# A transformer block on one core: feed-forward groups interleaved on VectorE, rounding constants made by ScalarE, the last group rounded in halves

## What is computed

```
x = x + attention(layernorm(x) * gamma + beta)     # x: 4 x 1024 x 128, 16 heads of 64
y = layernorm(x)
gate, up = q(y) @ q(w_gate).T, q(y) @ q(w_up).T    # 128 -> 352, twice
h = silu(gate) * up
x = x + q(h) @ q(w_down).T                         # 352 -> 128
```

## Time and profile before

| what | us |
| --- | --- |
| median of 3 runs (1539.41 to 1540.51) | 1540.29 |
| profiled execution, its own time | 1539.5 |
| its span, first to last instruction | 1537.7 |
| PE busy | 1458.0 (95%) |
| DVE busy | 1159.8 (75%) |
| ACT busy | 896.4 (58%) |
| POOL busy | 1346.2 (88%) |
| mean granted PE clock (1 is 2.4 GHz) | 0.983 |

### The profile page before, as it was taken

How to read it: one execution, slowest core, us unless ns; L and a number is a source line. 1 busy time by engine, 2 the same in 40 slices (tenths; PEclk the granted TensorE clock), 3 DMA queues, 4 the chain that set the end, 5 groups by cost and what they waited for, 6 DMA issues and landing times.

```text
span 1537.7 us, 28203 instructions
## 1 busy us (share of the span) xinstructions
PE 1458.0 (95%) x10537; PEld 771.2 (50%) x10537; DVE 1159.8 (75%) x1566; ACT 896.4 (58%) x1384; POOL 1346.2 (88%) x789
## 2 busy tenths in 40 slices
PE   4799999999999999999999999999999999997677
PEld 2345555555555455555555455555555455553455
DVE  7887777777777777777778777777777778754786
ACT  1366666666666666766566666666666656663222
POOL 3599999889889899999889899999889899975774
PEclk9899999999999999999999999999999999999898
DMA  5211121112111121111211111122112111100001
GB/s 142 48 37 49 36 50 50 41 50 49 49 45 33 45 50 35 50 41 49 49 49 45 36 43 49 36 50 48 42 50 50 45 45 33 31 25 16 7 14 35
DMA packets 69207, 67.26 MB, mean 44 GB/s; under 512 B 26512, under 2 KB 52432, under 8 KB 69072
## 3 DMA queue, kind: packets, MB, share of 16 engines
q1 hardware_dynamic: 69072, 65.46, 17.0%
HBM read 29.25 MB, written 2.62 MB: 21 GB/s over the span
## 4 chain that ended last, share of the span: by engine, by line
PE 87%; DVE 8%; issue 2%; ACT 2%; POOL 1%; DMA 0%; SPq 0%; ACTq 0%; DVEq 0%; POOLq 0%
PE po L1169 28%; PE st L1156 24%; PE mx L1217 11%; PE ms L1197 8%; PE ms L1234 4%; PE ms L1182 4%; PE ms L1245 4%; PE ms L1225 1%; PE mx L1304 1%; PE st L1304 1%; DVE probs L848 1%; DVE negmax L893 1%; DVE st L842 1%; POOL psum_keys L398 1%; DVE probs L1061 1%
## 5 line engine op out<-in xcount | busy, mean ns | idle before, releaser
L398 POOL TENSOR_TENSOR psum_keys<-psum_keys,probs 128x1024 f32<-128x1024 f32 x256 | 610.0, 2383 | 72.8 <-ACT probs L659 50.6
L659 ACT ACTIVATE probs<-st 128x1024 f32<-128x1024 f32 x512 | 497.5, 1028 | 122.3 <-PE st L1156 117.9
L893 DVE TENSOR_REDUCE negmax<-mx 128x2 f32<-128x1024 f32 x322 | 393.4, 1222 | 121.3 <-PE mx L1217 121.0
L1169 PE MATMUL po<-probs,v 128*64 128x512 f32 x2048 | 483.5, 593 | 0.0
L895 DVE TENSOR_REDUCE negmax<-mx 128x1 f32<-128x512 f32 x186 | 128.6, 692 | 183.4 <-PE mx L1217 183.4
L1169 PEld LDWEIGHTS po<-probs,v 128*64 128x64 f32 x2048 | 141.7, 137 | 218.9 <-issue 164.3
L1217 PE MATMUL mx<-keys_hi,queries_hi 64*128 64x512 f32 x1016 | 231.6, 452 | 13.8 <-DVE negmax L893 6.9
L1156 PE MATMUL st<-queries_lo,keys_hi 64*128 64x512 f32 x1024 | 201.9, 391 | 0.0
L1156 PE MATMUL st<-queries_hi,keys_hi 64*128 64x512 f32 x1024 | 201.7, 390 | 0.0
L1156 PE MATMUL st<-queries_hi,keys_lo 64*128 64x512 f32 x1024 | 201.7, 391 | 0.0
L1217 PEld LDWEIGHTS mx<-keys_hi,queries_hi 64*128 64x128 f32 x1016 | 95.8, 185 | 167.1 <-issue 124.8
(11 more groups left out here) (173 smaller groups left out, 1770.2 us busy)
## 6 DMA issues: line engine op xcount, KB each, us to landing
kq<-sin_part SPq DMA_DIRECT2D x256, 128.0 KB, 2.4
rsum<-recips SPq DMA_DIRECT2D x128, 128.0 KB, 2.9
wqkv<-in_L_attn_w_qkv_dram SPq DMA_DIRECT2D x32, 192.0 KB, 2.8
resid<-in_L_attn_x_dram SPq DMA_DIRECT2D x4, 512.0 KB, 8.1
wout<-in_L_attn_w_out_dram SPq DMA_DIRECT2D x32, 64.0 KB, 2.6
out_dram<-resid SPq DMA_DIRECT2D x8, 256.0 KB, 2.3
sums<-sums_kept SPq DMA_DIRECT2D x64, 4.0 KB
spread<-sums SPq DMA_DIRECT2D x64, 4.0 KB, 1.5
```

The lines of the kernel that those rows point to most:

```text
L398: nc.gpsimd.tensor_tensor(psum_keys[:, c], first, probs[:, (STEPS * P + i) % RING], ALU.add)\
L659: nc.scalar.activation(probs[:, step_n % RING], st[step_n % 2][:, :], ACT.Exp, scale=SCALE)\
L893: nc.vector.tensor_reduce(out, banks[:, :], AX.X, ALU.max, negate=True).then_inc(mx_free, 1)
L1169: last = mm(po[HD * a:HD * a + HD, :], v[:, P % 2, KEY_ORDER[jt], HD * a:HD * a + HD], probs[:, step_n % RING, a], start=(jt == 0), stop=( ...
```

## The change

- VectorE: the tiles of group g + 1 are put between the steps of group g: two tiles, the scales of g, two tiles, the values and exponents of g. The residual of group g - 3 is added before the scales.
- The exponents of h are a `tensor_tensor` with a mask column in PSUM (`h_mask`), broadcast over the columns, in place of a `tensor_scalar` with an immediate.
- The rounding constants of h are made by ScalarE with two instructions, `Relu(e - 1)` and `ROUND_C * that + ROUND_C`, whose biases are columns in SBUF (`rounding`). ScalarE signals `h_val_done`. In its queue they are the last thing of the next group.
- There are two tanh tiles in place of four, and four h buffers in place of three. `down` runs three groups behind in place of two, in halves of two tiles with `gate_and_up` of the next group between them; three groups of it are left at the end in place of two.
- `last_y` and `y_evac` of groups 6 and 7 move to between the halves of `down` in groups 5 and 6. `normalise_y` moves from ACT's group 2 to group 3, `maxima_y` and `reciprocals_y` behind the values of groups 2 and 3, and `last_exponents(7)` behind those of group 4.
- Group 7 is rounded by VectorE in two halves of 704 columns, and PE's last `down` starts after the first.
- The second reciprocal of pair 31 is taken before tiles 2 and 3 of group 0.

```diff
-    tanh_all = probs_flat[:, 0:GT * FFN]
-    h_all = [probs_flat[:, (1 + r) * GT * FFN:(2 + r) * GT * FFN] for r in range(3)]
+    tanh_tiles = [probs_flat[:, i * FFN:(i + 1) * FFN] for i in range(2)]
+    h_all = [probs_flat[:, 2 * FFN + r * GT * FFN:2 * FFN + (r + 1) * GT * FFN] for r in range(4)]
...
+    last_exp = st[1][:, :].rearrange("p c n -> p (c n)")[:, 0:2 * FFN]
+    h_mask, h_round = (halves[0][:, 2 * PART + i:2 * PART + i + 1] for i in range(2))
...
+        def constants_h(g, q):
+            if g == 0:
+                act.wait_ge(rounding_done, 1)
+            act.wait_ge(h_exp_done, g + 1)
+            nc.scalar.activation(h_exp[q], h_exp[q], ACT.Relu, bias=rounding[:, 0:1]).then_inc(h_two_done, 1)
+            act.wait_ge(h_two_done, g + 1)
+            nc.scalar.activation(h_exp[q], h_exp[q], ACT.Identity, bias=rounding[:, 1:2], scale=ROUND_C)\
+              .then_inc(h_val_done, 1)
+
         def group(g, q):
             gate_tanh(g, (2, 3))
-            if g == 2:
+            if g > 2:
+                copy_hT(g - 3, (0, 1))
+            if g in (GROUPS - 3, GROUPS - 2):
+                y_evac(g + 1)
+            if g == 3:
                 normalise_y(GROUPS - 2)
                 normalise_y(GROUPS - 1)
             if g < GROUPS - 1:
                 gate_tanh(g + 1, (0, 1))
-            if g > 1:
-                copy_hT(g - 2)
+            if g > 2:
+                copy_hT(g - 3, (2, 3))
+            if g > 0:
+                constants_h(g - 1, 1 - q)
...
+        def values(g, q):
+            link(scaled(h_all[g % 4], h_all[g % 4], GT * FFN // BLOCK, h_recip))
+            wide = [PART, GT * FFN]
+            nc.vector.tensor_tensor(h_exp[q].bitcast(I32), h_all[g % 4].bitcast(I32),
+                                    h_mask.bitcast(I32).broadcast_to(wide), ALU.bitwise_and).then_inc(h_exp_done, 1)
+
+        def own_rounding(g, q):
+            n = 2 * FFN
+            dve.wait_ge(h_exp_done, GROUPS)
+            link(nc.vector.tensor_scalar(h_amax, h_scale[:, q], 1.0, None, ALU.mult))
+            for half in range(2):
+                cols, blocks = slice(half * n, half * n + n), slice(half * n // BLOCK, (half + 1) * n // BLOCK)
+                link(nc.vector.scalar_tensor_tensor(last_exp, h_exp[q][:, cols], 1.0, h_round.broadcast_to([PART, n]),
+                                                    ALU.max, ALU.mult))
+                round_and_scale(h_all[g % 4][:, cols], last_exp, h_amax[:, blocks], n // BLOCK).then_inc(h_own_done, 1)
...
+        def group(g, q):
             if g < GROUPS - 1:
-                rounding_constants(h_exp[q]).then_inc(h_val_done, 1)
-            else:
-                link(rounding_constants(h_exp[q]))
+                gated(g + 1, (0, 1))
+            if g == 1:
+                output_half(1)
+            if g > 2:
+                add_residual(g - 3)
+            scales(g, q)
+            if g < GROUPS - 1:
+                gated(g + 1, (2, 3))
+            if g == 0:
+                filled(dve, ("S", PAIRS - 1, 1))
+            values(g, q)
+            if g == GROUPS - 1:
+                own_rounding(g, q)
                 add_residual(g - 2)
-                round_and_scale(h_all[g % 3], h_exp[q], h_scale[:, q], GT * FFN // BLOCK).then_inc(h_own_done, 1)
             if g == 1:
                 seed_shift(ln_rstd, batch_rows(BATCH - 1), BATCH + 2)
                 seed(ln_rstd, batch_rows(BATCH - 1))
+            if g == 2:
+                maxima_y(GROUPS - 2)
+                maxima_y(GROUPS - 1)
+            if g == 3:
+                reciprocals_y(GROUPS - 2)
+                reciprocals_y(GROUPS - 1)
             if g == 3:
                 last_exponents(GROUPS - 2)
+            if g == 4:
+                last_exponents(GROUPS - 1)
...
-        over_groups(gated)
+        gated(0, (0, 1))
+        nc.vector.memset(h_mask.bitcast(I32), EXPONENT)
+        nc.vector.memset(h_round, ROUND_C)
+        link(nc.vector.memset(rounding[:, 0:1], -1.0))
+        nc.vector.memset(rounding[:, 1:2], ROUND_C).then_inc(rounding_done, 1)
+        reciprocals(PAIRS - 1, 1)
+        gated(0, (2, 3))
+        output_half(0)
+        over_groups(group)
...
         def group(g, q):
             gate_and_up(g, (2, 3))
...
+            if g == 0:
+                output_projection(PAIRS - 1, 0)
+            if g > 2:
+                down(g - 3, (0, 1))
+            if g in (GROUPS - 3, GROUPS - 2):
+                last_y(g + 1)
             if g < GROUPS - 1:
                 gate_and_up(g + 1, (0, 1))
-            if g > 1:
-                down(g - 2)
+            if g == 1:
+                output_projection(PAIRS - 1, 1)
+                read_out(pe, ("O", PAIRS - 1, 1))
+            if g > 2:
+                down(g - 3, (2, 3))
...
-        down(GROUPS - 2)
-        down(GROUPS - 1)
+        for g in (GROUPS - 3, GROUPS - 2, GROUPS - 1):
+            down(g, range(GT))
```

More of the change, by code:

```diff
@@ L119, in block_program @@
     qscale = sb("qscale", [PART, 72])
+    rounding = sb("rounding", [PART, 2])
     wgT = sb("wgT", [PART, FFN])
@@ L750, in gate_tanh, with copy_hT @@
                 wait(act, gu_ps, n + 1)
-                nc.scalar.activation(tanh_all[:, t * FFN:(t + 1) * FFN], gate_up[n % 2][:, 0, 0:FFN], ACT.Tanh,
+                nc.scalar.activation(tanh_tiles[n % 2], gate_up[n % 2][:, 0, 0:FFN], ACT.Tanh,
                                      scale=0.5).then_inc(tanh_done, 1)
-        def copy_hT(g):
+        def copy_hT(g, tiles):
             kn = KSL[2][1]
-            for t in range(GT):
+            for t in tiles:
                 wait(act, hT_ps, GT * g + t + 1)
@@ L776, in _ @@
         gate_tanh(0, (1,))
-        over_groups(group, {4: lambda: y_evac(GROUPS - 2), 5: lambda: y_evac(GROUPS - 1)})
-        copy_hT(GROUPS - 2)
-        copy_hT(GROUPS - 1)
+        over_groups(group)
+        copy_hT(GROUPS - 3, range(GT))
+        copy_hT(GROUPS - 2, range(GT))
+        copy_hT(GROUPS - 1, range(GT))
     @block.vector
@@ L1046, in _, with gated, scales @@
         dve.wait_ge(key_part, 4 * PAIRS)
[L1049 to L1053, removed]
+        def gated(g, tiles):
+            for t in tiles:
+                n = GT * g + t
+                e, h = tanh_tiles[n % 2], h_all[g % 4][:, t * FFN:(t + 1) * FFN]
                 gate, up = (gate_up[t % 2][:, half] for half in range(2))
-                if t == 2 and g > 2:
-                    add_residual(g - 3)
-                if g == 0 and t == 1:
+                if t == 0:
+                    wait(dve, hT_ps, GT * (g - 3))
+                if n == 1:
                     dve.wait_ge(key_sum, keys_added(PAIRS, 0))
                     dve.wait_ge(pv_ps, STEPS * PAIRS)
-                wait(dve, tanh_done, GT * g + t + 1)
+                wait(dve, tanh_done, n + 1)
                 link(nc.vector.scalar_tensor_tensor(h, e, 1.0, gate[:, 0:FFN], ALU.add, ALU.mult))
                 nc.vector.scalar_tensor_tensor(h, h, 0.5, up[:, 0:FFN], ALU.mult, ALU.mult).then_inc(h_done, 1)
[L1063 to L1074, removed]
+        def scales(g, q):
             wait(dve, h_done, GT * g + GT)
@@ L1311, in transpose_h, with down @@
                 last = nc.tensor.transpose(hT_banks[t % 2][0:kn, c * PART:(c + 1) * PART],
-                                           h_all[g % 3][:, t * FFN + k0:t * FFN + k0 + kn], ident[:, :])
+                                           h_all[g % 4][:, t * FFN + k0:t * FFN + k0 + kn], ident[:, :])
             last.then_inc(hT_ps, 1)
[L1315 to L1326, removed]
+        def down(g, tiles):
+            if tiles[0] == 0:
+                if g < GROUPS - 1:
+                    pe.wait_ge(hq_done, g + 1)
+                if g < GROUPS - 2:
+                    wait(pe, y_done, g)
+                else:
+                    pe.wait_ge(h_done, GT * GROUPS)
+            for t in tiles:
+                if g == GROUPS - 1 and t % 2 == 0:
+                    pe.wait_ge(h_own_done, t // 2 + 1)
+                if t % 2 == 0:
+                    transpose_h(g, t)
                     transpose_h(g, t + 1)
@@ L1332, in down @@
                               start=(c == 0), stop=(c == 2))
-            last.then_inc(down_ps, 1)
+            if tiles[-1] == GT - 1:
+                last.then_inc(down_ps, 1)
         def last_y(g):
```

22 lines of the change are left out of this document (11 added, 11 removed).

## The result

| | before | after |
| --- | --- | --- |
| median, us | 1540.4 (4 runs, 1539.4 to 1540.7) | 1529.6 (4 runs, 1528.4 to 1530.6) |
| ratio to before | 1 | 0.9931, 95% interval 0.9913 to 0.9948 |
| span of the profiled execution | 1537.7 | 1528.8 |

Faster by 10.8 us, 0.7%, where 9.5 were forecast; 1531 against 1529.6. Lines of the changed kernel are shifted: its L1083 and L1084 are the old L1061 and L1062, L864 to L870 are L842 to L848, L873 and L883 are L851 and L861, POOL's L417 to L419 are L413 to L415, PE's L1362, L1369 and L1390 are L1304, L1311 and L1331. New are L1095, the exponents with the mask, and L773 and L775, ScalarE's constants.

The account below looks back on a forecast made before the run. It took the order of work between POOL and VectorE, neither full, as the limit. 6.4 later start - 12.1 of POOL's waits - 3.8 of tail = -9.5 us, so 1540.3 becomes 1530.8, said as 1531; range 1527 to 1537.

Parts of the forecast that it names:

- The chain: From POOL's first h rounding to the last residual add: 6.4 later start, 12.1 less waits, 3.8 less tail; -9.5 us.
- POOL's first rounding: Start of POOL's h roundings, behind group 0's constants on ScalarE: at 1425.3, 6.4 us later than 1418.86.
- the tail: From POOL's last rounding to the last residual add, two downs on PE: 12.5 us in place of 16.3.
- POOL's waits: POOL's waits during the h roundings, for seeds and for h and y constants: 6.6 us in place of 18.7.
- the walk: Step-by-step run through the engines' queues with estimated lengths; POOL ends at 1513.0, 5.7 us earlier.
- VectorE's group: VectorE's work on one h group with its residual add: 10.8 us, where a late, undisturbed group took 11.8.
- Cover for tanh: Values or scales between pairs of tiles: 3 us of VectorE work cover PE and tanh, about 1 short at 1.2 GHz.
- The new exponents: VectorE's tensor_tensor of 1408 columns with a PSUM mask: 1.6 us each, not held off by POOL.
- rival 2: New exponents held off by POOL, up to 3.2 us each, 8.5 in sum: 1539; 0.07 with other no-change ways.
- Rival 3: ScalarE's constants release POOL late; table loads cost 2.6 us per group, 10.3 in sum: 1541; 0.09 with other slower ways.
- rival 1: PE's holes of 2.5 to 5 us drop the clock, which takes back part: 1534 to 1537; chance 0.17.
- The last group in halves: VectorE's rounding of group 7 ends at 1516.4, before PE wants its first half at 1519.7; hidden.

Follow-up runs that it names:

- e1: Changed kernel with its new order kept, but exponents and constants of h by VectorE's tensor_scalar as before, none of it on ScalarE; 1533.8 us.
- e3: Changed kernel with the exponent mask column in SBUF in place of PSUM; 1537.8 us.
- e4: Changed kernel with a third ScalarE instruction per group, a Copy of 1408 columns of the constants onto themselves; 1533.7 us.
- e6: Changed kernel with unread matrix products of 512 columns in PE's two holes at the end, three and five of them; 1528.2 us.
- e9: Changed kernel with constants of groups 0 and 6 back on VectorE and POOL's rounding of group 6 in two halves of 704 columns; 1522.1 us.
- e5: Changed kernel with group 7 rounded by VectorE in one piece of 1408 columns, PE's last group waiting for the whole; 1530.1 us.
- e2: Kernel before with the offload alone: exponents by PSUM mask and constants by ScalarE for groups 0 to 6, old VectorE order; 1544.5 us.

## Why the prediction was right

Point by point, by its own steps:

- **The chain.** Three terms were given, and each came as forecast in kind and nearly in size: POOL's first rounding 6.3 us later against 6.4; its waits 13.3 less (17.8 to 4.6) against 12.1, which is all of the 13.3 by which the roundings are shorter; the tail 3.0 shorter against 3.8. Sum 10.05 against 9.5, and 10.8 in the medians. That it came within 0.6 us is in part luck: the gain in waits was forecast 1.2 too small and that in the tail 0.8 too large, and these two largely cancel.
- **POOL's waits.** 6.6 was forecast, 4.6 measured. Of the 2.0 us between them 0.5 is in the h constants (1.4 and 1.3 for groups 2 and 6, measured 1.0 and 1.2; 1.5 for group 5 as forecast). The other 1.5 is y: 1.0 and 0.9 were forecast, none and 0.4 measured. VectorE slipped in between two POOL instructions with both y 6 instructions at 1464.11, where the walk had it held off. The 18.7 of before was counted wrongly: 0.83 of it lies ahead of the first rounding, where the 99.8 begin. So POOL's work before was 99.8 - 17.8 = 82.0 and not 81.1, and with 86.5 - 4.6 = 81.9 after it did not change, as the prediction had said.
- **VectorE's group.** 10.8 us was the sum; the undisturbed group from 1481.52 (L864) to 1492.41 took 10.9. Cover for tanh was as argued: 19.6 us of waits became 4.1, of which 3.4 lie at tile 1, ahead of all of it. e1 prices the new order as a whole at 6.8 us (3.1 lost at the start, 6.2 won in the roundings, 3.6 in the tail); what the cover for tanh alone gives no run shows.
- **The new exponents.** Taken at L848's 1.62, measured 1.62, whatever POOL did. That L848 at 1506.00 was evidence for it was the right reading: e3 moved the one operand to SBUF and rival 2's time came true, 8.3 us where 8.5 had been priced. The near match is luck: the price was made of VectorE's waits for POOL, and the trace has 7.4 of the 8.3 in POOL's own instructions, held up by VectorE's.
- **ScalarE.** Two times 1.47, 3.0 us; no table load. Rival 3's slope was priced at up to four per microsecond, at four places. e4 measured three. If that slope held up to 2.6 us, the table loads would have cost 8 us and not 10, so rival 3, even had its condition held, would have ended some 3 us under the time of before, which a measurement hardly tells from it, and not above.
- **The clock.** The holes do cost, as rival 1 had it, and in the tail 0.8 more than the forecast had taken in: 5.7 us at half clock, where the walk had four. With tails of 12.4 to 12.6 four other kernels came to the forecast's 12.5, so the 0.8 is this execution's. e6 puts the whole price at 1.2 to 2.0 us. The walk took the clock as low after every hole of over 2 us, and rival 1 said that each hole from 2.5 us up is long enough to drop it. The traces are less regular: in the kernel after, the clock was 0.50 from 1420.0 to 1422.8, behind a hole of 2.47 us, but 1.00 from 1430.4 to 1433.0, behind one of 2.33, and in e9 it was 1.00 from 1436.6 to 1439.0, behind one of 3.09.
- **The last group in halves** was costed at nothing, hidden under PE's two other groups; e5 bears it out to within the scatter.

What was not seen: the offload is by itself a loss (4.5 us lost in e2), and it wins only behind the other part; and that VectorE's instructions lengthen POOL's, by 3.1 us in e1 and 7.4 in e3, where the prediction knew only the hold of VectorE by POOL.

## What to carry to other kernels

When two engines hand work to each other and neither is full, add up what the one waits for after its first instruction: that sum, and not a busy share, is what a new order can win (17.8 us here, of which 13.3 were won and 6.3 given back at the start). Where GpSimd is kept full, keep VectorE off the forms that GpSimd holds off and that hold it off: an operand in PSUM, even one column of constants broadcast, turned a `tensor_tensor` of 2.5 to 3.5 us into one of 1.62. Split the piece that the tail waits for and not the one next to it: halving VectorE's group 7 gave nothing, halving POOL's group 6 gave 3.4 us in the medians, 4.3 in the stretch, and kept TensorE's clock up without unread products.

## What the runs showed that I had not expected

- The hold works against GpSimd as well: in e3 its L420, 2.59 us long, took 3.85 in five of seven groups, each time when VectorE's exponents had come in between two of its instructions. This, and not VectorE's lateness, makes up most of what e3 costs.
- In e5 a VectorE add of 1408 columns with two SBUF inputs took 3.42 us under POOL's last instruction; in the kernel after, the same add in two halves with PSUM constants took 0.89 us each, the first of them (1510.16) under the same POOL instruction.
- ScalarE at 44% of the stretch had a slope of three: a queue in order with short cover is a bound long before it is full.
- Where the clock rises in the tail moved the tail by up to 1.1 us between executions of kernels alike there, as much as some of the effects studied; one execution's last add is no scale for them.
